# Weighing the values of 32 latent heads: from 26 products by quarters of query tiles to 15 by halves and parity

## The chip, the core and the metric

The kernel runs on one core of a Trainium2 chip. The metric is the time of one execution in microseconds (us), as the device measures it; the time of a kernel is the median of several executions.

## The reference

The reference is a decoder of four layers on x of shape (2, 1024, 256). Each layer adds a cross attention over a short context and then a feed-forward part, each scaled by a tanh gate. The change lies in the last feed-forward part, which has an attention of its own over the whole sequence (latent width 128, 16 heads of 8 columns, causal):

```python
c = rmsnorm(x, g1) @ w_down
q, k, v = rope(split(c @ wq)), rope(split(c @ wk)), split(c @ wv)
scores = einsum('bhqd,bhkd->bhqk', q, k) / sqrt(8)
scores = where(causal, scores, -inf)
attn = softmax(scores, axis=-1)
o = einsum('bhqk,bhkd->bhqd', attn, v)
x = x + o @ w_up
```

With two batches there are 32 pairs of batch and head, called heads below, each with a triangle of 8 query tiles by 8 key tiles of 128. After it a router sends each token to two of eight experts.

## The kernel before, in words

Five engine programs are written out by hand (`pe_program`, `act_program`, `dve_program`, `pool_program`, `sp_program`, L3077 to L3164) and are ordered by semaphores alone. Each engine works through its own list in order. The stage of the change is `pe_latent` (L2617), `act_latent` (L2753), `dve_latent` (L2866), `pool_latent` (L2986) and `sp_latent` (L2530). It goes head by head (`for h in range(HEADS + 1)`) and inside a head by key tile (`for j in range(TB)`, TB = 8). In iteration (h, j) the parts of three heads are interleaved:

- `exponentials(h, j)`: PE makes the scores of key tile j, transposed, keys on partitions (L2653, bfloat16 parts, plus the causal mask, L2656), and ACT exponentiates them into `expT` (L2774). A head has 12 pieces of at most 512 query columns (`PIECES`). They go round a ring of three PSUM banks, 4, 5 and 7 (`ring_plan`, `ring_bank`). `pe_ring_wait` makes PE wait until the use of the ring that lies three places back has been read.
- `score_maximum(h + 2, j)`: PE makes scores with queries on partitions for query tile j of the head after next (L2632, L2634; 128 columns at j = 0, 1024 at j = 7), in PSUM banks 0 to 3, and DVE reduces them to the maximum (L2885). PE waits before use n for the reduce of use n - 2.
- `maxima_rows(h + 1)` at j = 4: the maxima are turned (L2641), copied by ACT (L2764) and sent by DMA into the operand of the next head.
- `weigh(h - 1, ...)` at j = 1, 2 and 3: PE multiplies the exponentials with `head_values`, 8 columns of values, one column of ones (so that the sum of the weights comes out beside the outputs) and 23 of zeros. The stationary operand has 32 columns, so a product fills a quarter of the array and writes 32 of the 128 partitions of bank 6. Here part c (0 to 3) takes the query tiles c and 7 - c. For each key tile j and each part there is one product, of both query tiles (256 columns, L2673) or of the later one alone (128 columns, L2676): 26 products. The key tiles go as (0, 1), (2, 3), (4 to 7) at the three places.
- at j = 4 ACT copies the result (256 columns) out of bank 6 (L2788) into one of two buffers `sums`; at the start of j = 6, in the order of the code behind all that belongs to j = 5, PE turns it with two transposes (`divide`, L2684) into the other half of bank 6; at j = 6, after `score_maximum`, DVE divides by the sums of the weights: a reciprocal (L2891) and a product (L2894) into `attended`, which ends with an increment of `divided`.
- some (h, j) with j = 1 or 5 carry one step of the work on the other batch (`STEP_OF`, `pe_step`, `act_step`, `dve_step_of`), which also uses the ring.

POOL copies the values of head h into one of two `head_values` buffers once head h - 2 has been weighed (L3063) and splits the maxima (L3045 to L3053). SP issues the loads of the operands.

The matmuls in float32 show in the trace as two records each. These records are called passes below.

Of the kernel before, what the change touches and what calls it, by code (L numbers as in the profile page):

```python
# [64 lines left out]
def build(nc, ctx, a, out):  # L65
# [1933 lines left out]
    def sp_results(sp, r, y_rows):  # L1999
        sp.wait_ge(rows_stored, 32 * (r + 1))  # L2000
        if r == 1:
            sp.wait_ge(inner_added, 1)
        for s in range(3):
            sp.wait_ge(results_sent[s], 16 * uses_before(r, s, TOTALS[r], 3))
        for q in range(0, NT, 4):
            for k in range(r + 1):
                at = P * (1 + k * NT + q)
                sp.dma_start(backs()[k][:, q:q + 4, :],
                             y_rows[at:at + 4 * P].rearrange("(t p) d -> p t d", p=P)).then_inc(back_landed[q // 4], 16)
# [388 lines left out]
    sums = Kflat[:, 4096:4096 + 2 * D].rearrange("p (n c) -> p n c", n=2)  # L2398
# [47 lines left out]
    def ring_plan():  # L2446
# [8 lines left out]
        return uses  # L2455
# [19 lines left out]
    def pe_ring_wait(pe, use):  # L2475
# [5 lines left out]
        if what == "max":  # L2481
            pe.wait_ge(maximum_kept, h + 1)
        elif what == "step":
            pe_step_taken(pe, h)
        else:
            pe.wait_ge(exp_made, len(PIECES) * h + i + 1)
# [75 lines left out]
    def pe_step(pe, u):  # L2562
# [31 lines left out]
        elif kind == "Y":  # L2594
            pe.wait_ge(step_kept, kept(STEP_AT["T", b, i // 2]))
            for t in range(2):
                place = 2 * i + t if i < 2 else TB - 1 + TG - 2 * i - t
                at = place % TG
# [18 lines left out]
    def pe_latent(pe):  # L2617
# [41 lines left out]
        def weigh(h, lo, hi):  # L2659

            p = h % 2
            if lo == 0:
                pe.wait_ge(exp_made, scored_by(h))
                pe.wait_ge(values_taken, h + 1)
                if h >= 1:
                    pe.wait_ge(divided, h)
            for j in range(lo, hi):
                rows_of_j = expT[:, p, start[j]:start[j] + S - j * P].rearrange("p (t q) -> p t q", q=P)
                for c in range(HALF_T):
                    out_ = psum[32 * c:32 * c + 32, 6, 0:D]  # L2670
                    lhs, last = head_values[:, p, j, :], TB - 1 - c
                    if j <= c:
                        ins = pe.matmul(out_.rearrange("p (t q) -> p t q", q=P), lhs, rows_of_j[:, c - j:last - j + 1:last - c, :],  # L2673
                                        start=(j == 0), stop=(j == c), skip_group_check=True)
                    elif j <= last:
                        ins = pe.matmul(out_[:, P:2 * P], lhs, rows_of_j[:, last - j, :], start=False, stop=(j == last),  # L2676
                                        skip_group_check=True)
# [3 lines left out]
        def divide(h):  # L2681
            pe.wait_ge(sums_kept, h + 1)
            for n in range(2):
                ins = pe.transpose(psum[:, 6, D + n * P:D + (n + 1) * P], sums[:, h % 2, n * P:(n + 1) * P], ident[:, :])  # L2684
# [9 lines left out]
        for h in range(HEADS + 1):  # L2694
            for j in range(TB):
                if j == 6 and h >= 1:
                    divide(h - 1)
# [4 lines left out]
                if h >= 1 and 1 <= j <= 3:  # L2702
                    weigh(h - 1, *((0, 2), (2, 4), (4, 8))[j - 1])
                if j == 4 and h + 1 < HEADS:
                    maxima_rows(h + 1)
                if (h, j) in STEP_OF:
                    pe_step(pe, STEP_OF[h, j])
        for u in range(46, len(LATENT_STEPS)):
            pe_step(pe, u)
# [43 lines left out]
    def act_latent(act):  # L2753
# [24 lines left out]
        for h in range(HEADS + 1):  # L2778
            for j in range(TB):
# [4 lines left out]
                if h >= 1 and j == 4:  # L2784
                    act.wait_ge(head_weighed, h)
                    if h >= 3:
                        act.wait_ge(sums_turned, h - 2)
                    act.copy(sums[:, (h - 1) % 2, :], psum[:, 6, 0:D]).then_inc(sums_kept, 1)  # L2788
# [77 lines left out]
    def dve_latent(dve):  # L2866
# [19 lines left out]

        def divide(h):
            p = h % 2
            o = psum[:, 6, D:2 * D].rearrange("p (t c) -> p t c", c=32)
            dve.wait_ge(sums_turned, h + 1)  # L2890
            dve.reciprocal(shares[:, p, :], o[:, :, HD3]).then_inc(dve_step, 1)  # L2891
            dve.wait_ge(dve_step, vs())
            at = h % H * HD3
            dve.tensor_tensor(attended[:, h // H, :, at:at + HD3], o[:, :, 0:HD3],  # L2894
# [334 lines left out]
```

## Time and profile before

| | us |
|---|---|
| three runs | 3418.02, 3429.24, 3427.18 |
| median | 3427.18 |
| the profiled execution: its own time | 3428.99 |
| its span, first to last instruction | 3427.7 |
| mean granted TensorE clock | 0.952 of full speed |

The profile is of one execution. Its parts: busy time of each engine; the span in 40 slices; the chain of work that ended last; groups of instructions by line with their count, busy time, mean duration in ns and the idle time before them; DMA. Engines are PE (TensorE; PEld are its weight loads), DVE (VectorE), ACT (ScalarE), POOL (GpSimd), SP. A mean duration contains the latency of an instruction, so that records of one engine overlap; how fast they follow each other is read from their starts. The granted clock is 1.00 at 2.4 GHz and 0.50 at 1.2 GHz.

### The profile page before, as it was taken

What the parts mean: (1) busy time and instruction counts of PE and PEld (TensorE: products, weight loads), DVE (VectorE), ACT (ScalarE), POOL (GpSimd) and SP (SyncE); (2) the same over time, 40 slices, a digit from 0 to 9 for tenths busy, and PEclk for the clock granted to TensorE, in tenths of its full rate; (3) what the DMA queues carried; (4) which work ended last, traced back from release to release, by engine and by line L of the source; (5) the groups of instructions that cost most, each with busy time, mean ns of one, the idle gap of its engine ahead of it and who ended that gap; (6) DMA issues with size and microseconds to landing.
All of it is one profiled execution on the core that took longest, in us unless ns stands there. A gap on an engine that the chain in (4) does not pass through costs nothing.

```text
span 3427.7 us, 38700 instructions
## 1 busy us (share of the span) xinstructions
PE 3141.8 (92%) x14674; PEld 2176.6 (64%) x14674; DVE 1853.4 (54%) x3026; ACT 1190.0 (35%) x2206; POOL 629.9 (18%) x958
## 2 busy tenths in 40 slices
PE   7989899999999999999999998779978699995996
PEld 5668677677667767776666665655647544553564
DVE  5986788568666855773211015643236556665213
ACT  4333323542463255222222212321224345552332
POOL 1206301000100010011100002320434321111453
PEclk9999999999999999999999998879989979997998
DMA  5100100010010001000100000002730011011633
GB/s 133 59 1 1 52 1 1 13 64 1 1 52 25 1 13 42 23 1 1 49 13 25 1 0 19 1 13 106 245 120 1 20 32 44 29 42 73 223 115 110
DMA packets 85390, 150.95 MB, mean 44 GB/s; under 512 B 26357, under 2 KB 62743, under 8 KB 80471
## 3 DMA queue, kind: packets, MB, share of 16 engines
q1 hardware_dynamic: 70327, 77.15, 7.3%
q0 software_dynamic: 14880, 71.33, 6.0%
q8 instruction: 119, 1.95, 0.2%
q14 instruction: 64, 0.52, 0.1%
HBM read 173.14 MB, written 17.56 MB: 56 GB/s over the span
## 4 chain that ended last, share of the span: by engine, by line
PE 77%; DVE 11%; DMA 3%; ACT 3%; issue 3%; POOL 2%; SPq 0%; ACTq 0%; POOLq 0%; DVEq 0%
PE psum L391 10%; PE psum L414 9%; PE psum L1576 6%; PE psum L1564 6%; PE psum L1238 6%; PE psum L1250 6%; PE psum L2055 4%; PE psum L2076 2%; DVE row L2885 2%; PE psum L685 2%; PE psum L381 2%; PE psum L936 2%; PE psum L427 2%; DMA L_results<-shared,prep 2%; PE psum L2209 2%
## 5 line engine op out<-in xcount | busy, mean ns | idle before, releaser
L391 PE MATMUL psum<-Vt,shared 128*128 128x256 f32 (+1 forms) x1600 | 368.1, 385 | 12.8 <-ACT shared L552 11.9
L391 PEld LDWEIGHTS psum<-Vt,shared 128*128 128x128 f32 (+1 forms) x1600 | 300.4, 192 | 69.2 <-issue 31.0
L414 PE MATMUL psum<-Kt,xnTt 128*128 128x512 f32 (+1 forms) x960 | 343.9, 508 | 0.5 <-ACT xnTt L497 0.5
L414 PEld LDWEIGHTS psum<-Kt,xnTt 128*128 128x128 f32 x960 | 179.4, 189 | 158.6 <-issue 153.4
L2885 DVE TENSOR_REDUCE row<-psum 128x1 f32<-128x128 f32 (+7 forms) x256 | 188.0, 754 | 124.3 <-PE psum L2634 122.1
L1250 PEld LDWEIGHTS psum<-expert_w,prep 128*128 128x128 f32 x1024 | 194.6, 190 | 78.1 <-issue 57.9
L1250 PE MATMUL psum<-expert_w,prep 128*128 128x256 f32 x1024 | 240.8, 379 | 0.0
L1238 PE MATMUL psum<-weights,expert_w 128*128 128x512 f32 x512 | 240.3, 593 | 0.0
L381 PE MATMUL psum<-ident,shared 128*128 128x128 f32 x1120 | 155.0, 289 | 76.1 <-POOL shared L808 62.3
L2774 ACT ACTIVATE prep<-psum 128x512 f32<-128x512 f32 (+3 forms) x384 | 171.3, 490 | 148.3 <-PE psum L2656 147.7
L1138 DVE SCALAR_TENSOR_TENSOR bias<-Kt,small,bias 128x1232 f32<-128x1232 f32 x96 | 149.2, 1554 | 129.7 <-ACT Kt L1122 128.4
L588 DVE TENSOR_REDUCE row<-shared 128x16 f32<-128x1232 f32 x112 | 160.6, 1434 | 107.6 <-ACT shared L506 70.3
L1596 ACT ACTIVATE prep<-psum,fside 128x512 f32<-128x512 f32 x128 | 88.0, 687 | 344.9 <-PE psum L1564 344.9
L1624 DVE TENSOR_TENSOR inner<-psum,inner 128x512 f32<-128x512 f32 x56 | 36.1, 686 | 308.2 <-PE psum L1576 308.2
L381 PEld LDWEIGHTS psum<-ident,shared 128*128 128x128 f32 x1120 | 132.6, 147 | 86.2 <-POOL shared L808 67.7
L245 POOL TENSOR_SCALAR root_v<-meanvar 128x8 f32<-128x8 f32 (+3 forms) x19 | 8.6, 455 | 929.5 <-DVE meanvar L223 929.5
L1299 ACT ACTIVATE prep<-psum,bias 128x512 f32<-128x512 f32 x128 | 88.0, 687 | 237.9 <-PE psum L1238 237.9
L615 DVE TENSOR_TENSOR shared<-psum,bias 128x1232 f32<-128x1232 f32 x80 | 115.2, 1440 | 92.8 <-PE psum L414 92.2
L2144 DVE TENSOR_TENSOR prep<-psum,prep 128x512 f32<-128x512 f32 x62 | 42.9, 692 | 212.0 <-PE psum L2055 191.9
L506 ACT ACTIVATE shared<-shared 128x1232 f32<-128x1232 f32 x80 | 98.5, 1231 | 169.4 <-DVE shared L585 169.4
L2632 PE MATMUL psum<-weights 72*128 72x512 bf16 (+3 forms) x384 | 112.5, 349 | 40.3 <-DVE row L2885 22.6
L585 DVE TENSOR_TENSOR shared<-shared,row 128x1232 f32<-128x1232 f32 x96 | 139.5, 1453 | 3.3
(399 smaller groups left out, 6028.0 us busy)
## 6 DMA issues: line engine op xcount, KB each, us to landing
expert_w<-in_L_xattn_Wf SPq DMA_DIRECT2D x16, 512.0 KB, 5.7
weights<-q_parts SPq DMA_DIRECT2D x32, 144.0 KB
weights<-k_parts SPq DMA_DIRECT2D x96, 48.0 KB
weights<-in_L_xattn_Wk SPq DMA_DIRECT2D x4, 1024.0 KB, 5.0
weights<-in_L_xattn_Wv SPq DMA_DIRECT2D x4, 1024.0 KB, 7.1
weights<-in_L_xattn_Wq SPq DMA_DIRECT2D x4, 1024.0 KB, 5.4
weights<-in_L_xattn_Wo SPq DMA_DIRECT2D x4, 1024.0 KB, 5.3
weights<-in_L_ffn_w SPq DMA_DIRECT2D x8, 512.0 KB, 4.8
```

The lines of the kernel that those rows point to most:

```text
L381: ins = pe.transpose(flat[0:rows, base + c * P:base + (c + 1) * P], prob[:, t % 2, c * P:c * P + rows], ident[:, :])
L391: ins = pe.matmul(o_bank(t), probT[0:rows, t % 2, c, :], Vt[0:rows, t // TB, c, :], start=(c == 0), stop=(c == CH - 1))
L414: ins = pe.matmul(flat[:, par * 3 * BANK + at:par * 3 * BANK + at + cols], xnTt[:, par, k, :], Kt[:, t // TB, k, src:src + cols], start=(k ...
L585: dve.tensor_tensor(Pb, src, negmax.unsqueeze(2).to_broadcast([P, H, S2]), ALU.add).then_inc(shifted, 1)
L588: dve.tensor_reduce(total, Pb, AX.X, ALU.add).then_inc(dve_step, 1)
L1138: dve.scalar_tensor_tensor(flat_bias, hinge[:, j % 2, :], wto[:, j:j + 1], flat_bias, ALU.mult, ALU.add).then_inc(hinge_added, 1)
L1238: ins = pe.matmul(bank, slot(s)[0][:, k, f * P:(f + 1) * P], xnT_of(g)[:, k, :], start=(k == 0), stop=(k == KD - 1))
L1250: ins = pe.matmul(y[:, t * D:(t + 1) * D], hidden[:, n % 4, t * P:(t + 1) * P], slot(s)[2][:, f, :], start=(n % GROUP_STEPS == 0 and t % 2 ...
L1564: ins = pe.matmul(bank, expert_slots[e % 4][:, at:at + P], xnT[:, k, g * GRP:(g + 1) * GRP], start=(k == 0), stop=(k == KD - 1))
L1576: ins = pe.matmul(y[:, t * D:(t + 1) * D], hidden[:, n % 4, t * P:(t + 1) * P], expert_slots[e % 4][:, at:at + D], start=(f == 0 and t % 2 ...
L2774: act.activation(expT[:, h % 2, to:to + w], psum[:, ring_bank(("piece", h, i)), 0:w], ACT.Exp, scale=float(HD3) ** -0.5).then_inc(exp_made, 1)
L2885: dve.tensor_reduce(maxima[:, h % 2, t:t + 1], flat[:, base:base + cols], AX.X, ALU.max).then_inc(maximum_made, 1)
```

## The change

Bank 6 is used whole. The parts of the array are now (half n of the query tiles) times (parity of the key tile j). Half 0 has the query tiles 0, 1, 6, 7, half 1 the tiles 2, 3, 4, 5. The product of key tile j and half n writes the partitions from 32 * (2n + j % 2) on, up to 512 columns. Per head these are, in this order, in units of one query tile (128 columns):

| key tile | products: half 0 | half 1 |
|---|---|---|
| 0 | 4 | 4 |
| 1 | 1, then 2 | 4 |
| 2 | 2 | 4 |
| 3 | 2 | 3 |
| 4 | 2 | 2 |
| 5 | 2 | 1 |
| 6 | 2 | none |
| 7 | 1 | none |

The three places take the key tiles (0), (1, 2) and (3 to 7). What even and odd key tiles gave is now in different partitions and has to be added: ACT copies 512 columns in place of 256, into one buffer; PE makes four transposes in place of two, into a bank of the ring, for which `ring_plan` gets a use "turned" behind all else of j = 5; DVE adds the two parities with a `tensor_reduce` into `summed` ahead of the reciprocal and the product. The first sector that nothing writes is cleared once by DVE. PE now waits before its weighing for `sums_kept` where it waited for `divided`, and a use of the ring three places behind a "turned" waits for `divided`.

```diff
--- before.py
+++ after.py
@@ -1999,7 +1999,7 @@
     def sp_results(sp, r, y_rows):
         sp.wait_ge(rows_stored, 32 * (r + 1))
         if r == 1:
-            sp.wait_ge(inner_added, 1)
+            sp.wait_ge(inner_added, 2)
         for s in range(3):
             sp.wait_ge(results_sent[s], 16 * uses_before(r, s, TOTALS[r], 3))
         for q in range(0, NT, 4):
@@ -2395,7 +2395,11 @@
     Vflat = Vt[:, :, :, :].rearrange("p b c d -> p (b c d)")
     rope = Kflat[:, 0:2 * GRP].rearrange("p (m n c) -> p m n c", m=2, n=2)
     attended = Kflat[:, 2048:2048 + NT * L].rearrange("p (b t l) -> p b t l", b=B, t=TB)
-    sums = Kflat[:, 4096:4096 + 2 * D].rearrange("p (n c) -> p n c", n=2)
+
+    sums = Kflat[:, 4096:4096 + BANK]
+    summed = Kflat[:, 1024:1024 + 2 * TB * (HD3 + 1)].rearrange("p (n t c) -> p n t c", n=2, c=HD3 + 1)
+    QUERY_TILES = ((0, 1, 6, 7), (2, 3, 4, 5))
+    place_of = {t: 2 * i + n for n, tiles in enumerate(QUERY_TILES) for i, t in enumerate(tiles)}
     qkT = Vflat[:, 0:2 * S].rearrange("p (n c) -> p n c", n=2)
     split = Vflat[:, 2 * S:2 * S + PARTS * S].bitcast(BF16).rearrange("p (n a c) -> p n a c", n=2, a=PARTS)
     fed_rows = (xn, shared[:, 4096:4096 + 2 * D].rearrange("p (t d) -> p t d", t=2))
@@ -2452,7 +2456,9 @@
                     uses.append(("max", h + 1, 0))
                 if (h, j) in STEP_OF:
                     uses.append(("step", STEP_OF[h, j], 0))
-        return uses
+                if j == 5 and h >= 1:
+                    uses.append(("turned", h - 1, 0))
+        return uses + [("turned", HEADS - 1, 0)]
 
     RING = ring_plan()
     RING_AT = {use: u for u, use in enumerate(RING)}
@@ -2482,6 +2488,8 @@
             pe.wait_ge(maximum_kept, h + 1)
         elif what == "step":
             pe_step_taken(pe, h)
+        elif what == "turned":
+            pe.wait_ge(divided, h + 1)
         else:
             pe.wait_ge(exp_made, len(PIECES) * h + i + 1)
 
@@ -2594,8 +2602,7 @@
         elif kind == "Y":
             pe.wait_ge(step_kept, kept(STEP_AT["T", b, i // 2]))
             for t in range(2):
-                place = 2 * i + t if i < 2 else TB - 1 + TG - 2 * i - t
-                at = place % TG
+                at = place_of[2 * i + t] % TG
                 ins = pe.matmul(bank[:, t * D:(t + 1) * D], turned_outputs(i // 2)[:, at * P:(at + 1) * P], w_up, start=True, stop=True)
         elif kind == "G":
             pe.wait_ge(rows_ready, NT + TB * b + 2 * i + 2)
@@ -2662,26 +2669,39 @@
             if lo == 0:
                 pe.wait_ge(exp_made, scored_by(h))
                 pe.wait_ge(values_taken, h + 1)
+                pe.wait_ge(inner_added, 1)
                 if h >= 1:
-                    pe.wait_ge(divided, h)
+                    pe.wait_ge(sums_kept, h)
             for j in range(lo, hi):
-                rows_of_j = expT[:, p, start[j]:start[j] + S - j * P].rearrange("p (t q) -> p t q", q=P)
-                for c in range(HALF_T):
-                    out_ = psum[32 * c:32 * c + 32, 6, 0:D]
-                    lhs, last = head_values[:, p, j, :], TB - 1 - c
-                    if j <= c:
-                        ins = pe.matmul(out_.rearrange("p (t q) -> p t q", q=P), lhs, rows_of_j[:, c - j:last - j + 1:last - c, :],
-                                        start=(j == 0), stop=(j == c), skip_group_check=True)
-                    elif j <= last:
-                        ins = pe.matmul(out_[:, P:2 * P], lhs, rows_of_j[:, last - j, :], start=False, stop=(j == last),
-                                        skip_group_check=True)
+                lhs = head_values[:, p, j, :]
+
+                def query_tiles(n, first, t, count):
+
+                    to = 32 * (2 * n + j % 2)
+                    at = start[j] + (t - j) * P
+                    return pe.matmul(psum[to:to + 32, 6, first * P:(first + count) * P], lhs, expT[:, p, at:at + count * P],
+                                     start=(j < 2 and first == j * (1 - n)), stop=(j >= 4), skip_group_check=True)
+
+                if j == 0:
+                    ends = expT[:, p, 0:12 * P].rearrange("p (n c) -> p n c", n=2)[:, :, 0:2 * P]
+                    ins = pe.matmul(psum[0:32, 6, :].rearrange("p (n c) -> p n c", n=2), lhs, ends, start=True, stop=False,
+                                    skip_group_check=True)
+                else:
+                    if j == 1:
+                        query_tiles(0, 1, 1, 1)
+                    ins = query_tiles(0, 2, 6, 2) if j < 7 else query_tiles(0, 3, 7, 1)
+                if j < 6:
+                    lo_ = max(j, 2)
+                    ins = query_tiles(1, lo_ - 2, lo_, 6 - lo_)
             if hi == TB:
                 ins.then_inc(head_weighed, 1)
 
         def divide(h):
+            use = ("turned", h, 0)
+            pe_ring_wait(pe, use)
             pe.wait_ge(sums_kept, h + 1)
-            for n in range(2):
-                ins = pe.transpose(psum[:, 6, D + n * P:D + (n + 1) * P], sums[:, h % 2, n * P:(n + 1) * P], ident[:, :])
+            for n in range(TG):
+                ins = pe.transpose(psum[:, ring_bank(use), n * P:(n + 1) * P], sums[:, n * P:(n + 1) * P], ident[:, :])
             ins.then_inc(sums_turned, 1)
 
         for t in range(TB):
@@ -2693,18 +2713,18 @@
             score_maximum(1, t)
         for h in range(HEADS + 1):
             for j in range(TB):
-                if j == 6 and h >= 1:
-                    divide(h - 1)
                 if h < HEADS:
                     exponentials(h, j)
                 if h + 2 < HEADS:
                     score_maximum(h + 2, j)
                 if h >= 1 and 1 <= j <= 3:
-                    weigh(h - 1, *((0, 2), (2, 4), (4, 8))[j - 1])
+                    weigh(h - 1, *((0, 1), (1, 3), (3, 8))[j - 1])
                 if j == 4 and h + 1 < HEADS:
                     maxima_rows(h + 1)
                 if (h, j) in STEP_OF:
                     pe_step(pe, STEP_OF[h, j])
+                if j == 5 and h >= 1:
+                    divide(h - 1)
         for u in range(46, len(LATENT_STEPS)):
             pe_step(pe, u)
         pe_counts(pe, 1, srow(0, NT * E).rearrange("p (t e) -> p t e", e=E))
@@ -2783,9 +2803,9 @@
                     maxima_rows(h + 1)
                 if h >= 1 and j == 4:
                     act.wait_ge(head_weighed, h)
-                    if h >= 3:
-                        act.wait_ge(sums_turned, h - 2)
-                    act.copy(sums[:, (h - 1) % 2, :], psum[:, 6, 0:D]).then_inc(sums_kept, 1)
+                    if h >= 2:
+                        act.wait_ge(sums_turned, h - 1)
+                    act.copy(sums, psum[:, 6, :]).then_inc(sums_kept, 1)
                 if (h, j) in STEP_OF:
                     act_step(act, STEP_OF[h, j])
                 if (h, j) in SPLIT_AT and SPLIT_AT[h, j][1] % 2 == 0:
@@ -2884,14 +2904,21 @@
                 dve.wait_ge(maximum_split, h - 1)
             dve.tensor_reduce(maxima[:, h % 2, t:t + 1], flat[:, base:base + cols], AX.X, ALU.max).then_inc(maximum_made, 1)
 
+        dve.wait_ge(step_taken, taken(15))
+        dve.wait_ge(step_kept, kept(15))
+        dve.memset(psum[32:64, 6, 0:P], 0.0).then_inc(inner_added, 1)
+
         def divide(h):
             p = h % 2
-            o = psum[:, 6, D:2 * D].rearrange("p (t c) -> p t c", c=32)
+            o = psum[:, ring_bank(("turned", h, 0)), :].rearrange("p (t n c) -> p t n c", n=2, c=32)
             dve.wait_ge(sums_turned, h + 1)
-            dve.reciprocal(shares[:, p, :], o[:, :, HD3]).then_inc(dve_step, 1)
+            dve.tensor_reduce(summed[:, p, :, :], o[:, :, :, 0:HD3 + 1].rearrange("p t n c -> p t c n"), AX.X,
+                              ALU.add).then_inc(dve_step, 1)
+            dve.wait_ge(dve_step, vs())
+            dve.reciprocal(shares[:, p, :], summed[:, p, :, HD3]).then_inc(dve_step, 1)
             dve.wait_ge(dve_step, vs())
             at = h % H * HD3
-            dve.tensor_tensor(attended[:, h // H, :, at:at + HD3], o[:, :, 0:HD3],
+            dve.tensor_tensor(attended[:, h // H, :, at:at + HD3], summed[:, p, :, 0:HD3],
                               shares[:, p, :].unsqueeze(2).to_broadcast([P, TB, HD3]), ALU.mult).then_inc(divided, 1)
 
         for h in range(2):
```

## Rows read from the trace of the kernel before

**Rows 1.** The page, parts 1 and 2: busy time and the 40 slices
```profile
PE 3141.8 (92%) x14674; PEld 2176.6 (64%) x14674; DVE 1853.4 (54%) x3026; ACT 1190.0 (35%) x2206; POOL 629.9 (18%) x958
...
PEclk9999999999999999999999998879989979997998
```

**Rows 2.** Windows view of the stage of the latent heads; columns as its first line says
```profile
core 0: us, PE busy (x) PEld busy (x) DVE busy (x) ACT busy (x) POOL busy (x), PEclk, DMA share, GB/s
2771.00:3117.00 346.00, 315.16 (x3086) 174.89 (x3084) 199.96 (x351) 183.38 (x448) 57.27 (x197) 0.95 0.11 33
```

**Rows 3.** Chain of waits in one head: start us, us, what
```profile
2943.05 0.07 PE psum L2634
...
2943.14 1.09 DVE row L2885
...
2944.52 1.23 DVE row L2885
...
2945.80 0.28 PE psum L2632
```

**Rows 4.** Groups of instructions by line, the same head alone
```profile
L2676 PE MATMUL psum<-prep,fside 128*32 128x128 f32 x32 | 2.3, 277 | 0.0
L2673 PE MATMUL psum<-prep,fside 128*32 128x256 f32 x20 | 2.1, 386 | 0.0
```

**Rows 5.** Timeline of PE, the same head: start us, us, engine, line
```profile
2935.83 0.28 PE L2632 MATMUL psum<-weights 72*128 72x256 bf16 x1 [0.49 <-DVE row L2885]
...
2936.10 0.64 PE L2673 MATMUL psum<-prep,fside 128*32 128x256 f32 x8
...
2937.10 0.39 PE L2653 MATMUL psum<-weights 75*128 75x512 bf16 x1
...
2939.53 1.06 PE L2676 MATMUL psum<-prep,fside 128*32 128x128 f32 x20
2940.53 0.39 PE L2653 MATMUL psum<-weights 75*128 75x512 bf16 x1
...
2943.53 0.22 PE L2634 MATMUL psum<-expert_w 128*128 128x128 bf16 x1
2943.90 0.38 PE L2653 MATMUL psum<-weights 75*128 75x512 bf16 x1
...
2945.02 0.34 PE L2653 MATMUL psum<-weights 75*128 75x384 bf16 x1
```

**Rows 6.** Groups by line and form, ACT and DVE: copies and reduces of near sizes
```profile
L2125 ACT COPY shared<-psum 128x512 f32<-128x512 f32 x62 | 36.4, 587 | 102.7 <-PE psum L2064 99.3 <-PE psum L2076 1.8 <-issue 1.5
L2788 ACT COPY Kt<-psum 128x256 f32<-128x256 f32 x32 | 11.5, 360 | 2.3 <-PE psum L2676 2.3
...
L2885 DVE TENSOR_REDUCE row<-psum 128x1 f32<-128x256 f32 x32 | 13.6, 425 | 9.3 <-PE psum L2634 9.2
L2885 DVE TENSOR_REDUCE row<-psum 128x1 f32<-128x128 f32 x32 | 9.0, 282 | 7.1 <-PE psum L2634 7.1
```

**Rows 7.** Timeline of DVE in the same head: the division
```profile
2944.15 0.20 DVE L2891 RECIPROCAL row<-psum 128x8 f32<-128x8 f32 x1
2944.38 0.23 DVE L2894 TENSOR_TENSOR Kt<-psum,row 128x64 f32<-128x64 f32 x1
```

**Rows 8.** Waits in the heads' stage: who waited for whom, us in total, times, longest
```profile
PEld psum L2684 <- ACT Kt L2788: 7.7, 18, 1.1
```

**Rows 9.** Windows view: stretches before and after a change of the clock
```profile
2804.50:2807.90 3.40, 2.30 (x18) 1.06 (x15) 3.23 (x7) 2.55 (x6) 0.21 (x1) 1.00 0.12 27
2807.90:2811.30 3.40, 3.40 (x22) 1.83 (x21) 0.43 (x1) 0.00 (x0) 3.10 (x7) 0.50 0.17 60
2893.20:2896.60 3.40, 2.74 (x25) 1.22 (x26) 3.02 (x6) 2.29 (x6) 0.45 (x3) 1.00 0.12 36
2896.60:2900.00 3.40, 3.40 (x53) 1.66 (x45) 0.95 (x3) 1.43 (x4) 0.57 (x3) 1.00 0.16 57
```


## The prediction

> **What bounds the kernel now.** I read the page first: PE is busy in 92% of the span, and the granted clock is at full speed but for a few places, some of them in the slices of this stage [rows 1]. The windows view narrows it: the stage of the heads takes 346 us, with PE busy in 315 of them, a mean clock of 0.95, and DVE and ACT at little more than half [rows 2]. At 0.95, some 35 us of the stage ran at 0.50 (0.05 x 346 / 0.5). A tenth of the span is at stake, and PE looks like the bound.
>
> The chain of waits in one head says more. It is not PE all round. From the score product that ends at 2943.1 it goes over to DVE: a reduce, the division, the 1024-column reduce, and back to PE at 2945.80 [rows 3]. The timeline of PE has the same: the 256-column product of L2632 starts at 2935.83 and again at 2945.80, so an undisturbed head takes 9.97 us, and PE stands still before it for DVE [rows 5]. So a head is a loop of two parts. From 2935.83 to 2943.1 PE works almost without a gap, weighing included: what is added to PE there lengthens the head by as much. From 2943.14 to 2945.80 DVE sets the time: what is added to the division lengthens it too.
>
> **The weighing itself.** In the three places it takes 1.00 us each (2936.10 to 2937.10, 2939.53 to 2940.53; the place between is alike) [rows 5]. The head has 32 passes of 128 columns and 20 of 256, of 277 and 386 ns [rows 4]. The difference, 109 ns, is what 128 columns cost at the full clock; the rest of a duration is latency, which the next pass covers. Eight passes of 256 columns lie in 0.64 us, and twenty of 128 in 1.06 [rows 5]: the four parts run side by side. A place therefore lasts as long as its fullest part. In units of 128 columns and passes, these are now 8, 8 and 8 (part 3 has two query tiles for each of the key tiles 0 and 1; part 0 in the last place has four key tiles with one tile, twice). 8 x 0.109 = 0.87 us, and 0.13 us go to filling and draining. The number of products is in no term.
>
> After: in the first place half 0 and half 1 of key tile 0 have 4 tiles each, so 8 units; two parts of the array are empty. In the second place the fullest parts are half 1 even and half 1 odd, 4 tiles each, 8 units. In the third, half 0 odd has 2 + 2 + 1 tiles: 10 units. So 26 units against 24, if each part goes on by itself. But where two products of one part follow each other (key tile 1: 1 tile, then 2), the next parts may have to wait until the second is taken. The trace of before has no such place. Counted with a product holding up those behind it until its part is on its last pass, the second place has 9 units, and 10 if every weight load keeps its place. I take 27, bounds 26 and 28: +3 x 0.109 = **+0.33 us** a head (0.22 to 0.44), x 32 = **+10.5 us** (7 to 14). The work is the same 36 tiles; it is less even.
>
> **Copy and transposes.** ACT copies 512 columns for 256: 587 against 360 ns [rows 6], +0.23. The transposes waited for this copy 18 times [rows 8], in the heads without a step at j = 5; in the others the step covers it. 18 x 0.23 = **+4 us** (0 to 7.4, were it all hidden or none). Two more transposes of 128 columns, 0.109 each: 0.22 x 32 = **+7 us**. Both stand between the weighing and the products that start the DVE part.
>
> **Division and the new wait.** DVE gets a reduce of 144 elements. The nearest rows are 128 columns in 282 ns and 256 in 425 [rows 6]; I take 0.30, and 0.03 to the next instruction: +0.33 (up to 0.46). It lies in the DVE part of the loop. The second cost is larger: "turned" is followed in the ring by the pieces of j = 6 and 7, and the third use after it is the first piece of the next head. So this piece now waits for `divided`, and everything on PE's list is behind it: both pieces of j = 0, the scores of the head three on, the pieces of j = 1. The piece starts now at 2943.90 [rows 5], while the reciprocal starts at 2944.15 and the product at 2944.38 for 0.23 us [rows 7]. With the reduce before them the division ends at 2944.94, so the piece starts at about 2944.99, 1.09 late. The 384-column piece is 1.12 us behind it (2943.90 to 2945.02 [rows 5]), since it waits for the exponentials of the first. It would start at 2946.11 and stream 0.16 us, and the next L2632 would start at 2946.28 instead of 2945.80: +0.48 us. DVE alone would give +0.33; the two run beside each other, so the larger one counts. 30 heads have it: **+14.5 us** (10 with DVE alone, 19 with the reduce at its upper end). The cover used up here is PE's idle time before 2945.80.
>
> At nothing: the single memset of DVE, beside PE work at the start of the stage; the wait for `sums_kept` before the weighing, as the copy lies some 4 us earlier; one buffer `sums` for two, turned a head before; ACT's longer list (53% busy [rows 2]). No DMA moves.
>
> Sum: 10.5 + 4 + 7 + 14.5 = **+36 us** (24 to 47). An undisturbed head would go from 9.97 to 11.2 us.
>
> **The clock.** Where PE was busy in 2.74 of 3.4 us the clock stayed at 1.00 (2.4 GHz), where it was busy in 2.30 it went to 0.50 (1.2 GHz) for the next 3.4 us [rows 9]. Today PE has no record between 2943.75 and 2943.90; afterwards it stands still until 2944.99, 1.24 us in one piece, with the waits before the transposes and before L2632 on either side. This is more like the stretch that fell. A stretch of 3.4 us at half clock in PE's dense part costs 1.7 us. The 35 us now are ten such stretches; at most one in each of 31 heads gives 21 more, 36 us. I take half, 11, for **+19 us**, since a gap may fall either way.
>
> Total +55 us. The profiled execution took 3428.99 us (span 3427.7), 1.8 above the median 3427.18; the same sum on the median gives **3482 us**.
>
> **Rivals.**
>
> 1. The clock stays up: the gap is filled enough, as in the undisturbed heads now. For it: the stretches of [rows 9] do not tell which side 1.24 us is on. 3427 + 36 = 3463. Chance 0.28.
> 2. The clock falls in nearly every head, as each head gets the same gap. 3427 + 36 + 36 = 3499. Chance 0.16.
> 3. On the other side: the weighing costs by product, not by column. Then 15 for 26 takes 11/26 of 3.0 us = 1.27 a head, 41 us, in place of my +10.5: 36 - 10.5 - 41 = -15, 3412. It decides if a head saves over 0.8 us in the three places (25.5 / 32). Against it: the steps of 109 ns for 128 columns, and three places of equal length with 8, 8 and 10 products. Chance 0.06.
> 4. Passes do not overtake one another. Then a second product of a part stops all behind it, and the three places take 12, 18 and 16 units, 46 for 24: +77 us in place of 10.5, 3530. Against it: eight passes in 0.64 us are already closer than such an order allows. Chance 0.03.
> 5. The wait for `divided` costs nothing, because DVE finishes earlier or the piece is late anyway. Only 36 - 14.5 = +22 remains, 3449. Chance 0.05.
> 6. Waits elsewhere (operand loads, other steps) set the pace and absorb all: within 10 us of 3427. Against it: the undisturbed heads wait for DVE and ACT only. Chance 0.04.
>
> The Trainium skill, "TensorEngine Tiling (Array Packing)", Instruction Overhead, gives each matmul some 60 cycles of overhead. Worked out from that page, an estimate: 22 fewer passes a head at 25 ns are 0.55 us, 18 us in all, and the total would be 3464. It speaks for rival 3's side; the spacing of 109 ns for 128 columns shows none of it.
>
> The Trainium skill, "TensorE: Matmul & The Clock Gate", Part 3 (packing small matmuls), says that matmuls start and end in program order, with no reordering. This is rival 4's rule and would give its 3530; the eight passes in 0.64 us disagree with it for passes on different parts.
>
> **How the numbers follow.** The forecast (clock down in about half of the heads) has 0.38, own range 3470 to 3494. The range 3450 to 3512 takes in rivals 1 and 2 with the bounds of the terms. It leaves out 3, 4 and 6 and the lower side of 5, and the ends of 1 and 2, under 0.2 together. A measurement of this kernel tells about 0.3%, 10 us, from no change. Faster is rival 3: 0.06. Within 0.3%: 0.05 (rival 6, the edge of 3). Slower: 0.89.
>
> **What would show it.** In the profile after: 30 passes a head at the weighing, its three places at about 1.0, 1.1 and 1.2 us; L2653 at the first piece of a head released by DVE, some 1.1 us later after the reduce of 896 columns than now; an undisturbed head of 11.2 us; the transposes 0.23 us later behind ACT; the stage's clock below 0.95. Wrong would be: places that together take under 2.2 us (rival 3), heads of 10.8 us or less (the wait does not bind), a clock of 0.95 or more (rival 1), a place of two microseconds (rival 4).

## The result

The changed kernel takes 3478.66 us (median of 4 executions, 3474.16 to 3481.58), the kernel before 3423.36 beside it. The ratio is 1.0161, 95% interval 1.0144 to 1.0178: 55 us slower. The prediction was 3482 us (+55 on the median it started from), range 3450 to 3512. One of the six executions of the run more_dve below took 12652 us, and its time is the median of the other five.

### The profile page after: what moved, and what is told of

The parts are those of the page before. It is cut to its first block, busy times and chain, and to the rows that moved or that the text cites. A ratio compares the mean times of both kernels' runs of the same rounds, so it can differ in the third digit from the quotient of the medians.

```text
span 3480.3 us, 37518 instructions
## 1 busy us (share of the span) xinstructions
PE 3170.8 (91%) x14034; PEld 2178.3 (63%) x14034; DVE 1863.6 (54%) x3059; ACT 1195.5 (34%) x2206; POOL 626.5 (18%) x958
## 4 chain that ended last, share of the span: by engine, by line
PE 79%; DVE 10%; ACT 4%; issue 3%; POOL 2%; DMA 2%; SPq 0%; ACTq 0%; DVEq 0%; POOLq 0%
PE psum L391 10%; PE psum L414 9%; PE psum L1576 6%; PE psum L1564 6%; PE psum L1238 6%; PE psum L1250 6%; PE psum L2055 6%; PE psum L2076 3%; PE psum L685 2%; PE psum L2682 2%; PE psum L427 2%; PE psum L381 2%; PE psum L2660 2%; PE psum L936 2%; PE psum L2209 2%
## 5 line engine op out<-in xcount | busy, mean ns | idle before, releaser
L391 PEld LDWEIGHTS psum<-Vt,shared 128*128 128x128 f32 (+1 forms) x1600 | 301.0, 192 | 67.9 <-issue 30.5
L2660 PE MATMUL psum<-weights 75*128 75x512 bf16 (+3 forms) x384 | 124.8, 357 | 43.5 <-DVE Kt L2921 40.9
```

Of the source, the lines that this page charges most:

```text
L391: ins = pe.matmul(o_bank(t), probT[0:rows, t % 2, c, :], Vt[0:rows, t // TB, c, :], start=(c == 0), stop=(c == CH - 1))
L2660: ins = pe.matmul(psum[:, bank, 0:w], heads[:, 1, s, j * P:(j + 1) * P], heads[:, 0, s, at:at + w], start=True, stop=True)
```

## The profile after

The page, its head, busy times and granted clock:

```profile
span 3480.3 us, 37518 instructions
...
PE 3170.8 (91%) x14034; PEld 2178.3 (63%) x14034; DVE 1863.6 (54%) x3059; ACT 1195.5 (34%) x2206; POOL 626.5 (18%) x958
...
PEclk9999999999999999999999999879989699996998
```

PE has 640 matmul records fewer (14674 in [rows 1]) and is 29 us longer busy. The windows view of the heads' stage, with its first line for the columns:

```profile
core 0: us, PE busy (x) PEld busy (x) DVE busy (x) ACT busy (x) POOL busy (x), PEclk, DMA share, GB/s
2771.00:3160.00 389.00, 337.41 (x2411) 167.35 (x2408) 209.70 (x379) 190.12 (x447) 57.14 (x200) 0.91 0.09 30
```

The stage has grown from 346 us [rows 2] to 389, and the mean clock in it has gone from 0.95 to 0.91. The timeline of PE in one undisturbed head, to be laid beside [rows 5] (L2660 stands for L2653, L2639 for L2632, L2682 and L2687 for L2673 and L2676, L2704 for L2684):

```profile
2900.02 0.62 PE L2687 MATMUL psum<-prep,fside 128*32 128x512 f32 x1
...
2901.01 0.39 PE L2660 MATMUL psum<-weights 75*128 75x512 bf16 x1
...
2901.72 1.07 PE L2682 MATMUL psum<-prep,fside 128*32 128x128 f32 x10
2902.72 0.39 PE L2660 MATMUL psum<-weights 75*128 75x512 bf16 x1
...
2903.43 1.27 PE L2682 MATMUL psum<-prep,fside 128*32 128x256 f32 x16
2904.64 0.39 PE L2660 MATMUL psum<-weights 75*128 75x512 bf16 x1
...
2906.48 0.63 PE L2704 MATMUL psum<-ident,Kt 128*128 128x128 f32 x4 [0.40 <-ACT Kt L2808]
2906.94 0.28 PE L2660 MATMUL psum<-weights 75*128 75x256 bf16 x1
...
2908.11 0.22 PE L2641 MATMUL psum<-expert_w 128*128 128x128 bf16 x1
2909.62 0.39 PE L2660 MATMUL psum<-weights 75*128 75x512 bf16 x1 [1.29 <-DVE Kt L2921]
...
2910.75 0.34 PE L2660 MATMUL psum<-weights 75*128 75x384 bf16 x1
2910.93 0.28 PE L2639 MATMUL psum<-weights 72*128 72x256 bf16 x1
```

The three places take 0.99, 1.00 and 1.21 us (2900.02 to 2901.01, 2901.72 to 2902.72, 2903.43 to 2904.64) where they took 1.00 each. Thirty passes last longer than fifty-two did. The first piece of the next head, 2909.62, stands behind 1.29 us of idle PE, ended by DVE's L2921, the last product of the division. From L2639's 256-column product to the next it is 11.17 us (2899.76 to 2910.93), before 9.97. DVE and ACT in the same head:

```profile
2907.76 1.09 DVE L2905 TENSOR_REDUCE row<-psum 128x1 f32<-128x896 f32 x1 [0.61 <-PE psum L2641]
2908.76 0.30 DVE L2915 TENSOR_REDUCE Kt<-psum 128x72 f32<-128x144 f32 x1
2909.10 0.20 DVE L2918 RECIPROCAL row<-Kt 128x8 f32<-128x8 f32 x1
2909.34 0.23 DVE L2921 TENSOR_TENSOR Kt<-Kt,row 128x64 f32<-128x64 f32 x1
```

```profile
2905.76 0.57 ACT L2808 COPY Kt<-psum 128x512 f32<-128x512 f32 x1
```

The division is behind the 896-column reduce as before, with the new reduce of 0.30 us in front. Over the stage, the waits (total, times, longest) show the new one in 30 heads; before there was no such row:

```profile
PEld psum L2660 <- DVE Kt L2921: 50.7, 30, 2.8
PE psum L2660 <- DVE Kt L2921: 40.9, 30, 2.4
```

And the clock. Windows view of three stretches, from the stall at the end of the head that follows on (us, busy us of PE, PEld, DVE, ACT and POOL, then the granted clock):

```profile
2919.30:2922.70 3.40, 2.03 (x14) 0.84 (x14) 2.93 (x7) 1.45 (x4) 0.59 (x3) 1.00 0.20 63
2922.80:2926.10 3.30, 3.30 (x19) 1.10 (x15) 0.65 (x2) 1.30 (x4) 0.38 (x2) 0.50 0.07 25
2926.20:2929.50 3.30, 3.30 (x37) 1.71 (x31) 0.84 (x2) 1.25 (x3) 0.24 (x1) 1.00 0.00 0
```

PE was busy in 2.03 of 3.4 us, around the stall; the next stretch ran at 1.2 GHz, then the clock came back. The same pair, 2.30 of 3.4 and then 0.50, is in [rows 9]. Added up over short stretches of the windows view, from the first transposes of the stage to the last, PE ran at 1.2 GHz for 31 of 333 us before and for 61 of 379 us now. Where PE sets the time, half of such time is lost, so these 30 us more cost some 15 us.

## The experiments

Each ran beside executions of the kernel before on the same chip. The ratios are against these, with 95% intervals. Differences between two runs, in us, come out of the ratios within some 3 us of those of the times. Heads are undisturbed ones, from one 256-column score product to the next.

| run | us | ratio | undisturbed head, us |
|---|---|---|---|
| kernel before | 3422 to 3426 | 1 | 9.97 |
| the change | 3478.66 | 1.0161 (1.0144 to 1.0178) | 11.17 |
| w15 | 3430.38 | 1.0011 (1.0001 to 1.0021) | 10.12 |
| ring_wait | 3437.65 | 1.0036 (1.0022 to 1.0050) | 10.20 |
| bank6 | 3459.82 | 1.0103 (1.0088 to 1.0118) | 10.98 |
| early_divide | 3436.28 | 1.0028 (1.0017 to 1.0039) | 10.39 |
| split8 | 3481.44 | 1.0170 (1.0155 to 1.0186) | 10.95 |
| more_dve | 3438.58 | 1.0051 (1.0036 to 1.0066) | 10.31 |
| two_places | 3399.95 | 0.9935 (0.9920 to 0.9950) | 9.32 |
| one_place | 3391.99 | 0.9915 (0.9898 to 0.9931) | 8.92 |
| filled | 3448.39 | 1.0068 (1.0052 to 1.0084) | 11.17 |
| fifteen_one_place | 3404.71 | 0.9944 (0.9927 to 0.9961) | 9.30 |
| before_filled | 3416.74 | 0.9978 (0.9968 to 0.9987) | 9.97 |

### w15: the products alone

```diff
 kernel before
+ weigh() of the change, its places (0, 1), (1, 3), (3, 8)
- dve.reciprocal(shares[:, p, :], o[:, :, HD3])
+ dve.tensor_scalar(shares[:, p, :], o[:, :, HD3], TINY, None, ALU.max)
```

> The kernel before with the 15 products of the change and its three places alone; copy (256 columns), transposes, ring and wait stay those of before. The copied half holds only part of the sums, so the output is not the reference's, and an 8-element maximum stands for the reciprocal. Theory (cost by the fullest part of the array, parts independent of each other, 8 + 8 + 10 units of 109 ns): +0.22 us a head, an undisturbed head of 10.18 us, +7 us over the kernel before (about 3430 where that has 3423). If a second product of one part holds up the others: 27 or 28 units, +10 to +14 us. Rival (cost by product): 41 us faster than before, about 3382.

Measured 4 us over before (7 expected), an undisturbed head 10.12 us (10.18 expected). The timeline of PE:

```profile
2890.32 0.28 PE L2632 MATMUL psum<-weights 72*128 72x256 bf16 x1 [0.45 <-DVE row L2896]
...
2892.29 1.07 PE L2675 MATMUL psum<-prep,fside 128*32 128x128 f32 x10
2893.29 0.39 PE L2653 MATMUL psum<-weights 75*128 75x512 bf16 x1
...
2894.01 1.27 PE L2675 MATMUL psum<-prep,fside 128*32 128x256 f32 x16
2895.21 0.39 PE L2653 MATMUL psum<-weights 75*128 75x512 bf16 x1
...
2900.43 0.28 PE L2632 MATMUL psum<-weights 72*128 72x256 bf16 x1 [0.45 <-DVE row L2896]
```

The places have 1.00 us (2892.29 to 2893.29) and 1.20 us (2894.01 to 2895.21): what is longer is the one with 10 units in its fullest part. Eleven products fewer save nothing. Rival 3 of the prediction falls here.

### ring_wait: the wait alone

```diff
 kernel before
+                if j == 5 and h >= 1:
+                    uses.append(("turned", h - 1, 0))
...
+            use = ("turned", h, 0)
+            pe_ring_wait(pe, use)
             pe.wait_ge(sums_kept, h + 1)
```

> The kernel before with its two transposes put into a bank of the ring, and so with the wait of the next head's first piece for the division; 26 products, 256-column copy and the division without the reduce stay. Theory (chain of the wait): the division ends at 2944.61 in the traced head, the first piece starts 0.76 us late, the 256-column score product 0.15 us late: undisturbed head 10.12 us, +5 us in all, and more if the stall lets the clock fall (up to +20 more). Rival (the wait is free): within 3 us of before.

Measured 11 us over before and 10.20 us a head. The timeline of PE at the first pieces of two heads:

```profile
2893.79 0.39 PE L2657 MATMUL psum<-weights 75*128 75x512 bf16 x1 [0.95 <-DVE Kt L2900]
...
2903.99 0.39 PE L2657 MATMUL psum<-weights 75*128 75x512 bf16 x1 [0.95 <-DVE Kt L2900]
```

The wait alone makes PE idle for 0.95 us. The clock did not fall more often for it: the traced execution has 27 us at 1.2 GHz in the stage, before it is 31. The longer heads account for 7 of the 11 us (0.23 in 30 of them); the other 4 are not explained. The head is 0.08 longer than I expected. Here, as in the changed kernel, the transposes begin 0.14 us after ACT's copy ends; before they began 0.05 after it (copy 2941.65 for 0.36, the first piece of transposing 2942.06), and so they do in the run bank6, which has no ring wait ahead of them. So 0.09 us a head go with the move into the ring. It brings a second wait in front of the transposes, for a reader that had finished before, and another bank; I take it for the wait, but no run separates the two.

### bank6: the change without the ring's wait

```diff
 changed kernel
-                ins = pe.transpose(psum[:, ring_bank(use), n * P:(n + 1) * P], ...
+                ins = pe.transpose(psum[:, 6, n * P:(n + 1) * P], ...
-                    pe.wait_ge(sums_kept, h)
+                    pe.wait_ge(divided, h)
+                        pe.matmul(psum[32:64, 6, 0:P], parts16[:, 0, 32:64], ident16, ...
```

> The changed kernel without the ring's use and its wait: the four transposes go into bank 6, free since ACT's copy, and a product with zero weights clears the sector of tile 0. Everything else of the change stays. Theory: the first piece of a head is not held up, DVE alone sets the end of the loop: undisturbed head 11.0 us in place of 11.17, 5 us, and the clock no longer falls more often than before, some 20 us: about 3453. If the clock falls are not caused by this stall, only the 5 us: about 3473.

Measured 19 us less than the changed kernel. The head came out as expected, 10.98 us; the clock only in part, and the time is 7 us above the forecast (20 us of clock expected, from the 61 us at 1.2 GHz only 41 are left, against 31 before). The timeline of PE:

```profile
2893.70 0.28 PE L2635 MATMUL psum<-weights 72*128 72x256 bf16 x1 [1.11 <-DVE row L2900]
...
2904.68 0.28 PE L2635 MATMUL psum<-weights 72*128 72x256 bf16 x1 [1.11 <-DVE row L2900]
```

PE has no stall at the first piece now, but one of 1.11 us before L2635, the 256-column score product, for DVE's 1024-column reduce. Most of the idle time has moved, not gone: PE has 1.50 us without a record in an undisturbed head, 1.77 in the changed kernel. And the clock still fell (mean 0.94 between 2771 and 3100 us of the span, against 0.91 in the changed kernel and 0.95 before). So it is not this wait as such to which the clock answers.

### early_divide: one instruction group moved on DVE's list

```diff
 changed kernel, dve_latent
             for j in range(TB):
+                if h >= 1 and j == 6:
+                    divide(h - 1)
                 if h + 2 < HEADS:
                     score_maximum(h + 2, j)
...
-                if h >= 1 and j == 6:
-                    divide(h - 1)
```

> The changed kernel with DVE's division put ahead of the reduce of 896 columns instead of behind it, nothing else. Theory: the division fits mostly into DVE's idle 0.61 us before that reduce, ends near 2907.95 in the traced head, before the first piece needs it; the 1024-column reduce starts 0.55 us earlier and the next 256-column score product at 2910.2 in place of 2910.93: undisturbed head 10.4 us, 22 us off, and the clock's falls go too (20 us): about 3437. If the clock's falls stay: 3457. If DVE's order does not matter (PE and ACT set the head): 3479.

Measured 3436.28 us (3437 expected), and 10.39 us a head:

```profile
2898.17 0.28 PE L2639 MATMUL psum<-weights 72*128 72x256 bf16 x1 [0.40 <-DVE row L2905]
...
2908.56 0.28 PE L2639 MATMUL psum<-weights 72*128 72x256 bf16 x1 [0.40 <-DVE row L2905]
```

The idle time before L2639 is 0.40 us. The mean clock of the stretch 2771 to 3100 is 0.97. Four fifths of the loss of the change (a ratio of 1.0028 for 1.0161) hung on the place of three small instructions on an engine that is busy in half of the span.

### split8 and more_dve: two terms by themselves

```diff
 split8: changed kernel
-                    weigh(h - 1, *((0, 1), (1, 3), (3, 8))[j - 1])
+                    weigh(h - 1, *((0, 2), (2, 4), (4, 8))[j - 1])
 more_dve: kernel before, dve_latent divide()
+            dve.tensor_reduce(summed[:, p, :, :], both[:, :, :, 0:HD3 + 1]..., AX.X, ALU.add)
+            dve.wait_ge(dve_step, vs())
```

> The changed kernel with the key tiles at the three places as before, (0, 1), (2, 3), (4 to 7), nothing else. Theory (fullest part, parts independent): 8 + 8 + 8 units in place of 8 + 8 + 10, -0.22 us a head: 10.95 us where the changed kernel has 11.17, -7 us, 3472. Rival (cost by product: still 15): no change, 3479. If a product holds up those behind it, the first place grows to 9 or 10 units and less is gained.

> The kernel before with DVE's reduce of 144 elements added ahead of the reciprocal (its result is not used), nothing else. Theory: all of it lies in the part of the loop that DVE sets: +0.33 us a head, undisturbed head 10.30 us, +10 us over before, about 3436; more if the clock falls more often. Rival (hidden beside PE): within 3 us of before.

split8 is a miss in time and a hit in the head. An undisturbed head takes 10.95 us, 0.22 less, as 24 units for 26 say; the time did not go down at all, where 7 us were expected. The windows view of both kernels over the same stretch, first the changed one, then split8:

```profile
2771.00:3100.00 329.00, 287.48 (x2052) 144.71 (x2052) 184.71 (x336) 159.65 (x374) 51.92 (x175) 0.91 0.09 30
```

```profile
2771.00:3100.00 329.00, 287.09 (x2051) 140.52 (x2049) 185.33 (x335) 158.92 (x374) 49.07 (x169) 0.90 0.09 29
```

The mean clock went from 0.91 to 0.90. Added up over short stretches from the first transposes to the last, PE ran at 1.2 GHz for 85 us where it was 61 in the changed kernel: 24 us more, of which half, 12 us, are lost. That is more than the 7 us that the balance saves in 32 heads. The stall at the first piece is as long as before, 1.29 us, in a shorter head, so PE stands still for a larger part of it; that this makes the clock fall more often fits filled below, but no run holds it alone. more_dve gave +0.34 a head (+0.33 expected) and +16 us (+10 expected). The traced execution is the fastest of the five, 3431.80 us, with 20 us at 1.2 GHz in the stage; what the others lose is not shown. The reduce took 0.30 us, and the next instruction started 0.34 us after it:

```profile
2898.94 0.30 DVE L2893 TENSOR_REDUCE Kt<-psum 128x72 f32<-128x144 f32 x1
2899.28 0.21 DVE L2896 RECIPROCAL row<-psum 128x8 f32<-128x8 f32 x1
```

### two_places and one_place: the kernel before with fewer places

```diff
 kernel before
-                if h >= 1 and 1 <= j <= 3:
-                    weigh(h - 1, *((0, 2), (2, 4), (4, 8))[j - 1])
+                if h >= 1 and j == 2:
+                    weigh(h - 1, 0, 8)
```

(two_places has `1 <= j <= 2` and `((0, 2), (2, 8))`.)

> The kernel before, its 26 products in two places, key tiles (0, 1) and (2 to 7), in place of three; same products in the same order. Theory (fullest part plus 0.13 us for filling and draining at each place): 8 + 12 units, 2.44 us in place of 3.00: -0.56 us a head, 9.41 us, -18 us: about 3408. Rival (cost by product): only one filling and draining less, -0.13 us a head, -4 us.

> The kernel before, its 26 products all in one place, at j = 2. Theory: each part of the array has 9 tiles, 18 units, 1.96 + 0.13 = 2.09 us in place of 3.00: -0.91 us a head, 9.06 us, -29 us: about 3397. Less if ACT or DVE run dry during the 2 us. Rival (cost by product): -0.26 us a head, -8 us.

Measured 22 and 30 us less than before (18 and 29 expected). The heads are 0.09 and 0.14 us shorter than expected (9.32 and 8.92 us); why, no run shows. The timeline of PE of two_places, then of one_place:

```profile
2897.02 0.28 PE L2632 MATMUL psum<-weights 72*128 72x256 bf16 x1 [0.49 <-DVE row L2885]
...
2899.00 0.30 PE L2676 MATMUL psum<-prep,fside 128*32 128x128 f32 x2
...
2900.43 0.39 PE L2653 MATMUL psum<-weights 75*128 75x512 bf16 x1
...
2906.34 0.28 PE L2632 MATMUL psum<-weights 72*128 72x256 bf16 x1 [0.48 <-DVE row L2885]
```

```profile
2905.65 0.28 PE L2632 MATMUL psum<-weights 72*128 72x256 bf16 x1 [0.48 <-DVE row L2885]
...
2906.53 0.64 PE L2673 MATMUL psum<-prep,fside 128*32 128x256 f32 x8
...
2908.65 0.39 PE L2653 MATMUL psum<-weights 75*128 75x512 bf16 x1
```

The second place of two_places takes 1.43 us (2899.00 to 2900.43), 12 units and 0.12; the first takes 1.00 as before. In one_place all 52 passes take 2.12 us (2906.53 to 2908.65), 18 units and 0.16. The same products in the same order cost 3.0, 2.43 or 2.12 us by how evenly each place fills the four parts and how often it is entered. one_place beats both kernels.

### fifteen_one_place: the products of the change in one place

```diff
 early_divide
-                if h >= 1 and 1 <= j <= 3:
-                    weigh(h - 1, *((0, 1), (1, 3), (3, 8))[j - 1])
+                if h >= 1 and j == 2:
+                    weigh(h - 1, 0, 8)
```

> The changed kernel with DVE's early division and all 15 products in one place at j = 2. Theory (fullest part 10 tiles, 20 units, and one filling and draining instead of three): 2.31 us in place of 3.2: -0.91 us a head, undisturbed head 9.48 us where the early division alone had 10.39, -29 us from its 3436: about 3407. That stays above the 26 products in one place (3392), which have 18 units, a smaller copy and no reduce. Rival (cost by product): with 15 for 26 products it should beat 3392.

Measured 3404.71 us, 2 below the forecast, and 9.30 us a head where 9.48 were expected; its ratio of 0.9944 stands against 0.9915 for one_place, some 10 us. That difference contains the larger copy, the transposes and the reduce too. The products alone are in the timeline of PE:

```profile
2900.55 0.62 PE L2687 MATMUL psum<-prep,fside 128*32 128x512 f32 x1
...
2902.82 0.39 PE L2660 MATMUL psum<-weights 75*128 75x512 bf16 x1
```

The 30 passes take 2.27 us (20 units and 0.09) where the 52 of one_place took 2.12. With all products in one place, too, the 15 stay behind the 26.

### filled and before_filled: the clock by itself

```diff
 filled: changed kernel, pe_latent
+                if j == 7 and h >= 1:
+                    for _ in range(6):
+                        pe.matmul(psum[:, 6, P:4 * P], ident16, masks..., start=True, stop=True)
 before_filled: kernel before, between exponentials and score_maximum
+                if j == 1 and 1 <= h < HEADS:
+                    if h >= 2:
+                        pe.wait_ge(divided, h - 1)
+                    for _ in range(5):
+                        pe.matmul(psum[:, 6, 0:D], ident16, masks..., start=True, stop=True)
```

> The changed kernel with six products of 384 columns in bfloat16, whose results nobody uses, on PE's list between the last score product of a head and the first piece of the next, where PE stands still for the division (1.3 us in the traced head). Six take about 1.0 us, so they fit into the stall and an undisturbed head stays at 11.17 us. Theory (PE standing still lets the clock fall): the stage's time at half clock goes from 58 us back to some 27 as before, and the kernel gets faster by 15 to 20 us though it does more work: about 3462. Rival (the clock falls for another reason, or by chance): 3479 or slightly more.

> The kernel before with five products of 256 columns in bfloat16, whose results nobody uses, on PE's list where PE stands still before the 256-column score product (0.6 us in the traced head), behind a wait for the division of the head before last that is long over. Theory: they fit, an undisturbed head stays at 9.97 us, and the 27 us at half clock shrink to near nothing: about 13 us faster than before, 3412. Against the changed kernel with its own filling (3448) this leaves what the change costs apart from the clock: my sum said 36 us. Rival (the clock does not follow PE's stalls): 3425 or slightly more.

filled is 30 us faster than the changed kernel, where 15 to 20 were expected, with 192 products more on PE. The six fill most of the stall; the first piece comes 1.45 us after the start of the first of them, with 0.32 us idle:

```profile
2908.95 1.14 PE L2730 MATMUL psum<-expert_w 128*128 128x384 bf16 x6
2910.40 0.39 PE L2660 MATMUL psum<-weights 75*128 75x512 bf16 x1 [0.32 <-DVE Kt L2924]
```

The windows view of 2771 to 3100 us, the kernel before, ring_wait, filled and then before_filled:

```profile
2771.00:3100.00 329.00, 302.06 (x2927) 167.65 (x2925) 198.85 (x345) 174.91 (x426) 57.03 (x196) 0.95 0.11 35
```

```profile
2771.00:3100.00 329.00, 293.19 (x2886) 164.50 (x2878) 198.54 (x345) 171.70 (x420) 56.08 (x193) 0.96 0.11 35
```

```profile
2771.00:3100.00 329.00, 309.99 (x2359) 162.08 (x2357) 198.64 (x358) 170.82 (x401) 54.42 (x187) 0.99 0.11 35
```

```profile
2771.00:3100.00 329.00, 314.60 (x3165) 179.80 (x3158) 198.62 (x346) 181.55 (x443) 54.68 (x194) 0.99 0.11 34
```

The two filled kernels have a clock of 0.99. All that changed is that PE was busy while it waited, so the lower clock is shown to come from PE's standing still. In filled no time at 1.2 GHz is left between the first transposes and the last; the 61 us of the changed kernel would cost 30.5 us, and 30 were gained. I had expected that only what the change added would go, but the falls of before went too. Not every stall counts alike: ring_wait stands still for 1.2 us of each undisturbed head (the kernel before for 0.8, the changed one for 1.8), and its clock is no lower than before. before_filled gained 8 us on before, 13 expected.

## Why the prediction was right

**The loop.** PE from the 256-column score product to the last score product of the head, then DVE: this reading of [rows 3] held. I had 11.2 us for an undisturbed head; it is 11.17.

**Weighing, +0.33 us a head.** The rule was right (fullest part of the array, 109 ns a unit), the choice between its bounds was not. Parts go on wholly by themselves: 26 units, not 27. The three places sum to 3.20 us where they had 3.00, +0.20, a little under my lower bound of 0.22. w15 shows +0.15 in the head, as 0.04 of the idle time before the 256-column product goes (0.45 for 0.49 us), and +4 us in all, where I had 10.5 and 7 as the lower bound.

**Copy and transposes, +4 and +7 us.** The copy takes 574 ns (0.57 above), where I had 587. From the transposes to the next piece it is 0.46 us (2906.48 to 2906.94), before 0.28: +0.18 for 0.22. Not foreseen: the 0.09 us more between copy and transposes (ring_wait).

**Division and wait, +14.5 us.** The first piece starts 1.86 us after the 896-column reduce (2907.76 to 2909.62). I had 1.85 (2943.14 to 2944.99). The next L2639 is 3.17 us behind that reduce, before 2.66: +0.51 for 0.48.

**Sum.** 0.20 + 0.09 + 0.21 (copy) + 0.18 + 0.51 = 1.19, measured 1.20. Without the clock: filled is 22.5 us over its before, before_filled 8.2 under its own, so the change costs 31 us by work and waits. I had 36; the excess is about that of the weighing.

**Clock, +19 us.** The rest of 55 is 24 us, by the medians. The two traced executions are 53 us apart. Of these, the time at 1.2 GHz in the stage (61 us for 31, nine stretches of 3.4 us more where I had eleven) makes 15, work and waits in the stage make some 30, and some 7 lie outside the stage and are not explained. That the stall of PE brings the clock down was right, and filled shows it. The size was luck: I took half of the 21 heads that were left, and the stretches in [rows 9] did not tell. That the sum came out at 55 is luck too: work and waits came to 31 for 36, and the clock, by the medians, to 24 for 19. The traced run shows two heads in a row, one without a fall and one with it; L2639's 256-column product is at 2910.93, at 2922.09 (11.16 later) and at 2934.82 (12.73 later), and the stretch at 1.2 GHz above, from 2922.80, is in the second.

**Rivals.** Rival 1 (clock stays up) and 2 (falls in every head) lay on both sides of what came. Rival 3 is refuted by w15, and by 30 passes in 2.27 us against 52 in 2.12 (fifteen_one_place and one_place). Rival 4, and with it the strict order that the Trainium skill states ("TensorE: Matmul & The Clock Gate", Part 3), is refuted for passes on different parts: in the order of that rule the third place would take 16 units, 1.9 us, and it took 1.21. Rival 5 is refuted by the 30 waits for L2921 and by ring_wait (+11 us), rival 6 by the time itself. As to the overhead of each matmul that the Trainium skill gives ("TensorEngine Tiling (Array Packing)", Instruction Overhead), the 0.55 us a head for 22 fewer passes, an estimate worked out from that page, would have made w15 some 11 us faster than before (18 less the 7 of two more units); it is 4 slower.

The term that the prediction missed is not a cost but a choice: it named the cover that the division loses, but not that DVE has 0.61 us idle just before the 896-column reduce, into which the division could go (early_divide).

## What to carry to other kernels

Count a group of products on parts of the array by its fullest part, stretch by stretch, and not by the number of products: put them where every part has as much, and enter the group as seldom as the rest allows. When a result moves into a ring that the critical engine goes round, look which use comes three places behind it and whether its reader is late; then look for idle time on the reader's own list, since moving the reader cost nothing here. Where the bounding engine stands still in every round, read the granted clock of the stage beside the stall, and expect that a saving in its work can be taken back.

## What the runs showed of the hardware that I had not expected

- Transposes into a bank of the ring, with a second, fulfilled wait ahead of them, began 0.14 us after the copy that releases them, transposes into bank 6 with that one wait alone 0.05 us after it. Whether wait or bank makes the 0.09 us is open.
- Products whose results nobody uses made the changed kernel 30 us faster (3478.66 to 3448.39 us), and the kernel before 8 us, with the mean clock of the stage at 0.99 in both.
- A saving of 0.22 us in each head (split8) left the time where it was, 3481.44 against 3478.66 us, with 85 for 61 us at 1.2 GHz in the stage.
- Passes on the four parts of the array keep no order among one another: in the second place of the changed kernel the first pass of the last product started 26 ns after the first pass of the first one, while three passes of part 1 were still to start, and the place took 1.00 us, 8 units.
